# An attention product turned to tokens-by-features: narrow band as moving side, gate row from DRAM, residual added on GpSimd

## What is computed

```python
mod = (_silu(L0_c) @ L0_wmod).reshape(8, 6, 1, -1)
sa, ca, ga, sb, cb, gb = (mod[:, i] for i in range(6))
ga = (2 * (ga >= 0) - 1) * jnp.maximum(jnp.abs(ga), 0.25)      # gb the same
h = _layernorm(x) * (1 + ca) + sa
attn = jnp.einsum('ds,td->st', w1, w2) * sparse_mask           # 1024 x 1024
x = x + ga * gelu(jnp.einsum('bds,st->bdt', h, attn) + b2)
h = _layernorm(x) * (1 + cb) + sb
P = h @ U1;  gate, up = split(P @ V1 + b1)                      # rank 256, 2 x 2752 columns
x = x + gb * ((silu(gate) * up) @ U2 @ V2 + b2f)
```

## Time and profile before

| | us |
|---|---|
| median of 3 runs | 1242.93 (1242.53 to 1243.69) |
| the profiled execution, device time | 1241.24 |
| its span (first to last instruction) | 1239.5 |
| its mean granted PE clock | 0.988 of full speed |
| startup, up to the start of y(0) | 81.67 |
| y(0) to the start of y(2) | 93.89 |
| five iterations, y(2) to the start of y(7) | 194.10 |
| y(7) up to the second stage | 66.63 |
| the feed-forward stage | 803.21 |

### The profile page before, as it was taken

How to read it: one execution, slowest core, us unless ns; L and a number is a source line. 1 busy time by engine, 2 the same in 40 slices (tenths; PEclk the granted TensorE clock), 3 DMA queues, 4 the chain that set the end, 5 groups by cost and what they waited for, 6 DMA issues and landing times.

```text
span 1239.5 us, 15161 instructions
## 1 busy us (share of the span) xinstructions
PE 1186.1 (96%) x5617; PEld 950.3 (77%) x5617; DVE 669.8 (54%) x1049; ACT 407.0 (33%) x684; POOL 314.9 (25%) x257
## 2 busy tenths in 40 slices
PE   7788999999999899999999999999999999999997
PEld 4446678877786678888888888888888888888885
DVE  0838699999996643543444443443444444344343
ACT  0122334444443264413322323322332332332331
POOL 0023221332313176541211302203113122131110
PEclk9898999999999899999999999999999999999999
DMA  9796635535457454240131122104015014013001
GB/s 350 290 371 250 270 145 196 226 146 211 165 199 288 172 172 162 95 156 15 68 119 52 68 77 93 68 25 145 11 58 170 1 68 140 31 68 119 18 1 68
DMA packets 54145, 165.76 MB, mean 134 GB/s; under 512 B 4992, under 2 KB 9536, under 8 KB 52032
## 3 DMA queue, kind: packets, MB, share of 16 engines
q1 hardware_dynamic: 54080, 164.86, 36.3%
HBM read 122.84 MB, written 42.01 MB: 133 GB/s over the span
## 4 chain that ended last, share of the span: by engine, by line
PE 82%; DVE 9%; ACT 2%; issue 2%; DMA 2%; POOL 1%; SPq 1%; DVEq 0%; ACTq 0%
PE bank L498 25%; PE bank L500 24%; PE bank L499 24%; PE bank L568 4%; DVE nrm L1070 2%; PE bank L664 2%; DMA x<-in_x 2%; PE bank L533 2%; DVE bn L1228 1%; DVE h_lo L1171 1%; DVE bn L1060 1%; DMA wm_sb<-in_wmod 1%; POOL g L1349 1%; PE bank L804 1%; DVE xr L1223 1%
## 5 line engine op out<-in xcount | busy, mean ns | idle before, releaser
L1285 DVE SCALAR_TENSOR_TENSOR act<-bank,b_sb,act 128x512 f32<-128x512 f32 (+1 forms) x176 | 131.9, 750 | 382.4 <-PE bank L500 360.7
L996 ACT ACTIVATE act<-bank,b_sb 128x512 f32<-128x512 f32 (+1 forms) x176 | 121.1, 689 | 505.7 <-PE bank L500 504.5
L498 PE MATMUL bank<-pt,v_hi 128*128 128x512 f32 x688 | 268.7, 391 | 1.5 <-DVE act L1285 1.5
L499 PE MATMUL bank<-pt,v_hi 128*128 128x512 f32 x688 | 267.7, 389 | 0.0
L500 PE MATMUL bank<-pt,v_lo 128*128 128x512 f32 x688 | 267.7, 389 | 0.0
L1295 DVE TENSOR_TENSOR act_lo<-act,act_hi 128x512 fp32r<-128x512 f32 (+1 forms) x176 | 164.9, 937 | 0.2
L498 PEld LDWEIGHTS bank<-pt,v_hi 128*128 128x128 f32 x688 | 129.1, 188 | 31.2 <-issue 2.6
L500 PEld LDWEIGHTS bank<-pt,v_lo 128*128 128x128 f32 x688 | 129.2, 188 | 27.0
L499 PEld LDWEIGHTS bank<-pt,v_hi 128*128 128x128 f32 x688 | 129.2, 188 | 26.3
L1421 POOL TENSOR_TENSOR x2t<-gbb_bc,x2t 128x512 f32<-128x512 f32 x64 | 85.5, 1358 | 241.3 <-DMA x2t<-x_dram 241.3
L498 PE MATMUL bank<-act_hi,u_hi 128*128 128x512 f32 x336 | 130.8, 389 | 0.9 <-DVE act_lo L1295 0.9
(11 more groups left out here) (122 smaller groups left out, 1600.2 us busy)
## 6 DMA issues: line engine op xcount, KB each, us to landing
wm_sb<-in_wmod SPq DMA_DIRECT2D x10, 2048.0 KB, 11.1
xr<-in_x SPq DMA_DIRECT2D x16, 1024.0 KB, 6.8
x_dram<-xr SPq DMA_DIRECT2D x16, 1024.0 KB, 4.2
x2t<-x_dram SPq DMA_DIRECT2D x32, 512.0 KB, 4.0
out<-x2t SPq DMA_DIRECT2D x32, 512.0 KB, 4.9
xs<-in_x SPq DMA_DIRECT2D x7, 2048.0 KB, 7.7
pt_dram<-pt_st SPq DMA_DIRECT2D x8, 1024.0 KB, 3.9
pt<-pt_dram SPq DMA_DIRECT2D x8, 1024.0 KB, 5.8
```

The lines of the kernel that those rows point to most:

```text
L498: nc.tensor.matmul(acc, s_hi, m_hi, start=start, stop=False)
L499: nc.tensor.matmul(acc, s_hi, m_lo, start=False, stop=False)
L996: nc.scalar.activation(act[0:w, i % 2, :], bank[0:w, i % 2, :], ACT.Silu, bias=b1_sb[0:w, i, 0:1]).then_inc(silu_done, 1)
L1285: nc.vector.scalar_tensor_tensor(act[0:w, i % 2, :], up, b1_sb[0:w, i, 1:2], act[0:w, i % 2, :], ALU.add, ALU.mult).then_inc(act_done, 1)
```

## The change

The attention product is made tokens-by-features. For a token block n of 128 tokens and a half h of 512 features, `y(b, n, h)` takes `h1` as the stationary side (128 x 128) and columns of `attn` as the moving side, only those within REACH = 70 of block s. A half takes five blocks s, with 198, 268, 268, 198 and 70 columns (in the mirrored order for the other half), three matmuls each; a last matmul adds `beta` (the shift's product with `attn`, plus b2) by a stationary side `row_of` that picks the batch's row, 512 columns. The products use banks 0 to 3. So PE has 120 narrow and 8 wide matmuls where it had 66 wide, and no `turn_back`. Gelu has no bias, and writes into one of two slots of `g`. The gate is now a row along the features: it is stored to `ga_dram` once and for each batch loaded into `ga_bc` by a broadcast DMA (`gates_a_in`). POOL's `x2_block(b, n)` has two multiplies by `ga_bc` (line 1414) and two adds of the residual `xr` (line 1420); the add on DVE is gone. Gelu of token block n waits for `x2_ready` of block n - 2, since it takes that slot. `beta` is copied by ACT, its low part made by DVE, before y(0); eight small products add b2. The residual comes in four tiles, each issued once DVE has normalised that tile of the batch before; x2 is stored in four tiles. The iterations are written out instead of looped. Batch 0 loses its inner interleaving: y(0), then modulation products 4 and 5 and the turn of the gate, then the turns of h1(1). P(b - 1) alternates with the turns of h1(b + 1), and P(6) follows y(7) and the turn of the second gate. The narrow mask also narrows the products that make `attn` and the shift; off-band columns are more pieces. In the feed-forward stage the half block moves, for batches 1 to 7, from the end to the middle.

The core of the diff:

```diff
+    REACH = 70
+
     def band_cols(s):
-        return max(0, P * (s - 1)), min(D, P * (s + 2))
+        return max(0, P * s - REACH), min(D, P * (s + 1) + REACH)
...
-            g = buf(p1, "g", [P, FB, TOK])
+            g = buf(p1, "g", [P, 2, D])
+            ga_bc = buf(p1, "ga_bc", [P, D])
+            beta = buf(p1, "beta", [P, D], F32R)
...
+        BLOCKS = [list(range(IB))] + [list(range(IB // 2)) + [IB - 1] + list(range(IB // 2, IB - 1))] * (NB - 1)
...
+            def y(b, n, h):
+                acc = bank[:, 2 * (n % 2) + h, :]
+                toks = slice(n * P, (n + 1) * P)
+                if b > 0 or n >= 2:
+                    pe.wait_ge(gelu_done, b * 8 + 2 * (n - 2) + h + 1)
+                for part in near[h]:
+                    s, a, e = part
+                    if n == 0:
+                        pe.wait_ge(lo_ready, turn1(b) + s + 1)
+                    y_part(acc, h, toks, part, part == near[h][0])
...
+                nc.tensor.matmul(acc, row_of[:], beta[:, h * HALF:(h + 1) * HALF], start=False, stop=True,
+                                 skip_group_check=True).then_inc(y_done, 1)
+
+            def y_part(acc, h, toks, part, start):
+                s, a, e = part
+                cols = slice(a - h * HALF, e - h * HALF)
+                for t, (moving, weight) in enumerate(((h1_hi, attn_hi), (h1_hi, attn_lo), (h1_lo, attn_hi))):
+                    nc.tensor.matmul(acc[:, cols], moving[:, s, toks], weight[:, s, a:e], start=start and t == 0,
+                                     stop=False, skip_group_check=True)
```

More of the change, by code:

```diff
@@ new lines, in _ @@
+            mod_pair(4)
+            dve.wait_ge(ga_turned, 1)
+            nc.vector.tensor_copy(gate_rows[:], bank[0:FB * NB, 6, 0:P]).then_inc(ga_rows_ready, 1)
+            stats1(1, range(TT * NH))
+            aggregate1(1)
+            norm1(1)
+            for k in range(FB):
+                lo1(1, k)
+            for n in range(TT):
+                stats2(0, n)
+            norm2(0)
+            mod_pair(6)
+            stats1(2, range(TT * NH))
+            aggregate1(2)
+            mod_pair(8)
```

917 lines of the change are left out of this document (480 added, 437 removed).

## The result

The changed kernel takes **1352.7 us** (median of 4 runs, 1347.7 to 1356.9) where the kernel before takes 1242.7 (4 runs): 1.088 times as long, 95% interval 1.086 to 1.091. The forecast was 1303 with a range to 1333: the direction and the mechanism are the forecast's, the size is not, and the time lies outside the range. The profiled execution took 1351.07 us, its span 1349.1. Its runs differ more among themselves than those of before (0.7% against 0.1%).

What follows compares the result with a forecast made beforehand. It took the attention iterations to become bound by a ring of waits from the gate row's load, no longer PE. Startup +39, iterations +18.4, last batch +5.4, feed-forward -3 on 1241.24 gave 1301, as median 1303 us; range 1256 to 1333.

Steps and rivals of the forecast that it cites:

- the ring: Attention iteration: gate row's landing, POOL's blocks 0 and 1, rstd1, norm1, turns with U1 product; 42.5 us with hand-overs.
- rival C: Narrow attention matmuls hide no weight load, so each costs load plus stream: 1332 us, chance 0.12.
- rival A: Transfers of one queue share the engines, so the gate row lands early: 1265 to 1267 us, chance 0.18.
- 42.5: One attention iteration, set by waits from gate row to turns: 42.5 us, against 38.81 before; counted five times, +18.4.
- S + 13: Landing of the gate row in ga_bc, 13 us after S, the start of y(b), with transfers draining in order.
- beside a busy POOL 4.4: DVE's norm1 of the next batch while POOL works: 4.4 us, between 4.0 and 4.7.
- 13.3: Turns of h1 alternating with the U1 product on PE, at an iteration's end: 0.5 + 7 x 1.83 = 13.3 us.
- The bound of 45.5: Upper bound of an attention iteration: 1.36 us a POOL operation, norm1 4.7, gate row at S + 14.
- +39: Startup up to y(2): starts at 215 us against 175.56, delayed by gate rows and POOL's blocks; bounds +25 to +48.
- 72: Batch 7 up to the second stage, with product 11 waiting for its chunk: 72 us against 66.63, +5.4.
- -3: Feed-forward stage: half block in mid-batch removes 2.4 us of waits and shortens the end; -3 us (-4 to 0).
- B: Gate row never waits on anything, so PE sets iterations at 36.0 us: 1238 us in all, chance 0.08.

Runs made afterwards that it cites:

- In the experiment: DVE's statistics of x2 of batch 1 spread between its h2 and h1 work, against a kernel with both edits and a reordered startup: 1254.6 us.
- the kernel with both edits: Changed kernel with the gate row's load first on SP and POOL's blocks 2 and 3 held until norm1 is done: 1269.2 us.
- the last kernel: Kernel with rewritten startup, plus batch 7's chunk 11 loaded before two x2 stores and its product and turn one unit earlier: 1222.6 us.

## Why the prediction was wrong

The mechanism was right, the terms of the sum were not. Of the 49.4 us that are missing, 26.5 are three mis-sized terms of the iteration (the landing of the row, norm1 beside POOL, the turns on a PE at the lower clock), counted five times; 7.1 are an order in batch 1 that the forecast left out; 8.4 lie in batch 7, 6.4 in startup, 0.9 in the feed-forward stage.

**What held.** The bound moved from PE and DVE to the ring, in the forecast's order of links; the narrow matmuls cost what the forecast said (3.98 us a token block against 3.91, rival C is out: an unhidden load would have added 0.11 us to each); DVE is no longer nearly full (33.2 us of 47.8 busy, 69%), though one of its operations, norm1, is a link of the ring; the transfers drained in order (the 1 MB store landed at 290.1, the 512 KB row issued behind it at 291.4), so rival A is out, by the trace and by the run with the row one place earlier. The Trainium skill ("TensorE: Matmul & The Clock Gate", Part 3, The mechanism) has two statements on this: one sentence lets a load be pulled ahead of matmuls in flight when its row group does not conflict with theirs or when it goes to the background weight buffer, and a list item, the one that the forecast weighed, allows the overlap only when the row groups differ. The loads here are all full ones (128x128), and the 120 of an iteration were hidden, so the trace speaks against the list item; it fits the sentence, by way of the background buffer.

**The iteration, "42.5", measured 47.8.** Three terms of the sum were too small, none of them missing:
- The row: S + 13 in the forecast, S + 15.0 in the trace. The single drain times were right, but they were added from the first residual issue, and the residual tiles went out one by one behind norm2's tiles, the last near S + 3.2.
- norm1: "beside a busy POOL 4.4", measured 6.8. The 4.0 to 4.7 of the earlier trace rows are four tiles of which not all met POOL. In the kernel before POOL was done 2.0 us after norm1 began, and the four tiles took 1.11, 1.53, 0.80 and 0.80 us; in the changed kernel POOL works through all of it, and they took 1.75 to 1.77 each. The rows of norm1 and of POOL beside it, before (the first two) and after:

```profile
235.12 4.01 DVE L1070 TENSOR_SCALAR nrm<-xs,mv,rstd 128x1024 f32<-128x1024 f32 x4
234.64 2.49 POOL L1349 TENSOR_TENSOR g<-g,now_ga 128x512 f32<-128x512 f32 x2
...
302.60 6.81 DVE L1116 TENSOR_SCALAR nrm<-xs,mv,rstd 128x1024 f32<-128x1024 f32 x4 [0.62 <-POOL rstd L1406]
302.53 2.97 POOL L1414 TENSOR_TENSOR g<-g,ga_bc 128x512 f32<-128x512 f32 x2
305.46 3.39 POOL L1420 TENSOR_TENSOR xr<-g,xr 128x512 f32<-128x512 f32 x2
```

  So the forecast took a mean over tiles with and without a neighbour for the price beside a neighbour that never rests. Four tiles at the 1.53 of the slowest, 1.45 from start to start, would have been 5.9 us; the other 0.9 goes with POOL's operation on two full tensors, which is longer (1.24 us alone against 1.04). That division is an estimate from these rows; that POOL is the cause the experiment with POOL kept still shows: 3.0.
- The turns with the U1 product: 13.3, measured 14.7, because PE comes to them after waits and at the lower clock. The forecast named this and gave it a price only in startup. The clock was 0.89 in this window and 1.00 in the one without waits, and the same 242 matmuls took 37.5 and 34.1 us of PE's time. Not every wait costs this: in the 36.98 us iteration of the kernel with the row first PE waited once, 2.7 us, the eight transposes behind it took 1.09 us, and the clock stayed at 1.00.

Together 2.0 + 2.4 + 1.4 = 5.8, less 0.4 of POOL, 5.4: the 5.3 of the table to within 0.1. The bound of 45.5 took 4.7 for norm1 and a PE at full clock throughout; it held neither a POOL that works through all of norm1 nor the clock behind the waits.

**Iteration 2, "42.5", measured 54.95.** The forecast counted five iterations alike. In batch 1 DVE's order has all eight parts of h1(2) ahead of the statistics of x2(1), so that norm2(1) began 8.9 us after y(2), not 0.2 (timeline of DVE):

```profile
230.25 1.54 DVE L1116 TENSOR_SCALAR nrm<-xr,mv,rstd 128x1024 f32<-128x1024 f32 x2 [1.41 <-POOL rstd L1406]
...
276.49 1.53 DVE L1116 TENSOR_SCALAR nrm<-xr,mv,rstd 128x1024 f32<-128x1024 f32 x2
```

The residual is issued behind norm2, and the ring starts there. The failing step is the multiplication by five. Of the 12.4 us 8.7 are this order and 5.3 those of every iteration, 14.0, of which 1.6 did not come. In the experiment the order was worth 6.5 (42.3 against 35.8).

**Startup, "+39", measured +45.8.** y(0) came 2.75 us later than forecast. It then took 19.5 us from its first to its last matmul, where the kernel with both edits took 15.8 for the same matmuls. The windows of 92 to 112 us, of the changed kernel and of that one, differ in the clock (0.87 and 1.00):

```profile
92.00:112.00 20.00, 19.59 (x141) 16.86 (x143) 0.69 (x1) 3.67 (x5) 3.57 (x1) 0.87 0.33 121
```

```profile
92.00:112.00 20.00, 19.31 (x156) 15.62 (x155) 2.35 (x8) 3.67 (x5) 3.94 (x1) 1.00 0.48 171
```

These 3.7 us belong to the execution and not to the kernel: up to there the kernels are the same, and in the profiled executions of the kernels with the row one place earlier and with POOL kept still y(0) took 15.8 at a clock of 1.00 too (y(2) at 219.5 and 219.2), in that with the row first 18.9 at 0.87. So some 2 of the 6.4 us can't be laid to the forecast. The later steps kept about the same distance: the gate row landed at 130.3 (forecast 122.5), that of batch 1 at 186.9 (179), POOL's two blocks ended at 197 (189), y(2) at 221 (215). Two waits carry startup's length, ACT's for POOL's blocks and PE's behind them, in the timelines of ACT and PE:

```profile
135.41 1.08 ACT L927 ACTIVATE g<-bank 128x512 f32<-128x512 f32 x2 [34.26 <-POOL xr L1420]
```

```profile
143.03 1.33 PE L612 MATMUL bank<-ident,nrm 128*128 128x128 f32 x5 [15.11 <-DVE h_lo L1222]
```

**Batch 7, "72", measured 80.4.** The chunk landed 1.5 us late; from there to the start of U1 product 6 it took 13 us, not 7, of which 3.7 is PE waiting for the gate's clamping on DVE behind the last turn; the clock of the window was 0.85. Loading the chunk ahead of the stores of blocks 0 and 1 and moving its product and turn one unit forward took 6.9 us away.

**Feed-forward, "-3", measured -2.1.** The half block in the middle took away 3.1 us of waits (2.4 to 0.2, and the 0.9 at the very end), as forecast. Against it stands a wait that grew, which the forecast did not have: behind U1 product 7 PE stands 4.2 us for DVE's product of a block, before 1.5. The experiment with the old order has the 4.2 as well, so they don't come from the order.

```profile
PE bank L546 <- DVE act L1347: 4.2, 1, 4.2
```

Another 2.7 us are 12 matmuls that lie ahead of the stage's start in the changed kernel (3481 in the window, before 3493). -3.1, +2.7 and -2.7 make -3.1, against -2.1 measured: the step's size came out near the forecast's by terms that it did not have, which is luck. The last 1.0 is not shown; behind the wait of 4.2 us the wide matmuls started every 0.43 us for some 5 us.

**The rivals.** B (the row binds nowhere) is what the experiments built: it gives 34.1 us an iteration, not 36.0, and after the startup was rewritten 1222.6. The gain of the new form is real, 4.7 us an iteration, turn-backs and narrow band together; the changed kernel lost it, and 9 us more each time, to where one 512 KB load stood in a queue and to what POOL did beside DVE.

**What stays open.** The 13.8 us of standing in batch 1 of the rewritten startup, by what way POOL slows norm1, and why the runs of the changed kernel and of those made from it differ by up to 0.9% while before's differ by 0.2%. The granted clock differs between such runs (0.972 in the profiled execution of the last kernel, 1230.4 us, and 0.976 to 0.978 in the others), which fits, but no run separates it.

## What to carry to other kernels

When a value moves from a per-partition column that sits in SBUF to a row that is loaded for each iteration, find the place of that load in its queue and everything in front of it before counting what the new form saves; a load with a buffer that has long been free belongs at the head. Price an operation on DVE by a row in which POOL does what it will do then, and for as long: the neighbour changed the price by a factor of more than two here, and a mean over tiles of which only some met it hid that. And a wait on PE can be paid twice, once standing and once at the lower clock behind it, so the upper bound of a sum with new waits has to hold both.

## What the runs showed of the hardware

- DVE's subtraction and product over a tile of 1024 columns took 809 ns with POOL idle, 1.11 and 1.53 us for the two that met POOL multiplying by a column, and 1762 ns with POOL multiplying or adding full tensors without a pause; POOL's own operations took 1274 ns on average where it was kept still meanwhile, and up to 1.7 us each beside those tiles where it was not (1327 to 1385 on average over an iteration). Holding POOL back was worth 3.6 us an iteration in one kernel and 2.9 to 4.3 in the other.
- With 128 stationary columns and a new load for each matmul, three matmuls of 70 moving columns took 0.27 us and three of 198 took 0.31: a third of the columns for 0.87 of the time.
- A 512 KB broadcast of one DRAM row landed 4.0 us after its issue with the queue empty, 8.0 behind 2 MB of tiles that were issued in the 2.4 us before it, and 10.2 behind 3 MB issued in the 3.4 us before it.
- The same 242 matmuls of an iteration were 34.1 us of PE's time at a granted clock of 1.00 and 37.5 at 0.89, with waits of 7.5 and 2.8 us. One wait of 2.7 us in an iteration without the longer one left the clock at 1.00.
